# A Fourier-operator tokenizer whose spectra change their order in SBUF: the mix, the prelude and the pair loops

## The reference, cut to what matters

```
spec = DFT of every image, kept modes only (8 x 16 modes, 32 channels, re and im)
mix  = for each mode: spec[image, channels] x weights[mode]        # 128 modes
y    = inverse DFT of mix  +  3x3 convolution of the layer's input
h    = leaky(y + bias)                                             # next layer's input
```

## Time and profile before

| | us |
|---|---|
| median of three runs (lowest, highest) | 7572.34 (7569.57, 7587.36) |
| the profiled execution, its own time | 7572.24 |
| span of the profile | 7570.0 |

### The profile page before, as it was taken

The page is one execution under the profiler, slowest core; times in us unless marked ns, Lnnn a source line. Parts: engine busy times, 40 slices in busy tenths (PEclk is TensorE's granted clock), DMA queues, the critical chain, the costliest instruction groups (busy, mean ns, idle before and its releaser), DMA issues. The chain is left out here.

```text
span 7570.0 us, 260619 instructions
## 1 busy us (share of the span) xinstructions
PE 6734.3 (89%) x107382; PEld 4009.6 (53%) x107382; DVE 4997.2 (66%) x7931; ACT 2567.0 (34%) x4418; POOL 64.7 (1%) x47
## 2 busy tenths in 40 slices
PE   4699997999999899999989999758888888888888
PEld 3566666666666666666654444334444444444443
DVE  3499995777777477777657777665545545454554
ACT  1244442333333233333223333233343333433334
POOL 1000000000000000000000000000000000000000
PEclk8799998999999899999989999879999999999999
DMA  6666665444444444444432222200000000000000
GB/s 169 150 127 125 127 125 131 122 125 118 123 124 114 132 121 125 118 123 124 112 102 77 76 77 77 88 6 1 3 1 3 3 1 3 1 3 3 1 3 2
DMA packets 657148, 581.17 MB, mean 77 GB/s; under 512 B 328160, under 2 KB 527968, under 8 KB 649190
## 3 DMA queue, kind: packets, MB, share of 16 engines
q1 hardware_dynamic: 656776, 576.22, 31.0%
HBM read 328.55 MB, written 260.39 MB: 78 GB/s over the span
## 5 line engine op out<-in xcount | busy, mean ns | idle before, releaser
L554 PE MATMUL abank<-inv_basis,mode_tile 128*32 128x128 f32 x32768 | 1013.8, 276 | 84.9 <-DMA mode_tile<-m_img 56.6
L600 PE MATMUL zbank<-rows_in,conv_taps 64*32 64x512 f32 (+1 forms) x18432 | 1057.0, 588 | 6.1 <-issue 4.9
L554 PEld LDWEIGHTS abank<-inv_basis,mode_tile 128*32 128x32 f32 x32768 | 877.3, 111 | 259.8 <-issue 259.8
L961 DVE SCALAR_TENSOR_TENSOR rows_out<-zbank,conv_bias,work 128x1024 f32<-128x1024 f32 x512 | 633.9, 1279 | 524.9 <-PE zbank L609 510.0
L822 ACT ACTIVATE turned<-tbank 128x1024 f32<-128x1024 f32 x400 | 410.4, 1026 | 1560.3 <-PE tbank L623 1560.2
L816 ACT ACTIVATE inv_copy<-abank 128x1024 f32<-128x1024 f32 x512 | 524.4, 1024 | 766.6 <-PE abank L554 766.6
L638 PE MATMUL zbank<-fwd_basis,turned 128*64 128x128 f32 x12288 | 758.1, 276 | 19.4 <-ACT turned L822 14.7
L937 DVE TENSOR_TENSOR work<-inv_copy 128x512 f32<-128x512 f32 x1024 | 654.2, 685 | 155.1 <-ACT inv_copy L816 154.8
L638 PEld LDWEIGHTS zbank<-fwd_basis,turned 128*64 128x64 f32 x12288 | 666.5, 137 | 96.9 <-issue 96.9
L609 PE MATMUL zbank<-rows_in,conv_taps 32*32 32x512 f32 (+1 forms) x18432 | 702.5, 593 | 0.0
L600 PEld LDWEIGHTS zbank<-rows_in,conv_taps 64*32 64x32 f32 x18432 | 347.7, 106 | 578.5 <-issue 562.8
(11 more groups left out here) (367 smaller groups left out, 7103.8 us busy)
## 6 DMA issues: line engine op xcount, KB each, us to landing
h_rows<-rows_out SPq DMA_DIRECT2D x768, 256.0 KB, 4.0
rows_in<-h_rows SPq DMA_DIRECT2D x384, 512.0 KB, 4.9
m_img<-rows_out SPq DMA_DIRECT2D x32, 1024.0 KB, 5.4
mode_tile<-m_img SPq DMA_DIRECT2D x512, 64.0 KB, 2.9
rows_in<-x_slots SPq DMA_DIRECT2D x96, 194.9 KB
rows_out<-x_slots SPq DMA_DIRECT2D x96, 194.9 KB
x_slots<-x_pad SPq DMA_DIRECT2D x4, 3121.5 KB
tokens<-spectra SPq DMA_DIRECT2D x512, 4.0 KB
```

Of the source, the lines that this page charges most:

```text
L554: last = nc.tensor.matmul(ab[32 * p:32 * p + 32, s, 128 * k:128 * k + 128], mode_tile[u][:, k, a, :], inv[:, k, s, 128 * p:128 * p + 128], ...
L600: nc.tensor.matmul(section(zb[32 * p:32 * p + 32, 2 * a + so, :])[:, :, :, out], conv_t[part, dx, so, :], moving(part, p, 0, src), start=( ...
L961: nc.vector.scalar_tensor_tensor(out=rows_out[u][:, half].rearrange("p (s x) -> p s x", s=2), in0=zb[:, 2 * a:2 * a + 2, :], scalar=conv_b ...
```

## The change

1. `g_img` is ordered by mode: the 128 images of one mode are adjacent. The stationary operand of L773 becomes contiguous. The writers of `g_img` (L836, the expansion's copies L902 and L1063) write one word out of each 128.
2. The weights of mix step `a + 3` are asked for right after the store of step `a - 1`; in the first layer those of steps 1 to 3 ahead of the mix.
3. The last store of a mix is split: eight partitions first, with a semaphore of their own (`m_head`), and the modes of pair 0 wait for that head and for the seven stores ahead of it.
4. In the prelude each tile has a modes buffer of its own (in `rows_flat`), so L921 does not wait for stores; the grid's `x_modes` are asked for after tile 1.
5. The four copies to `x_slots` are gone. `x_rows` come straight from `x_pad`, as 12 transfers of 3 partitions in place of 3 of 12.
6. The pair loops have no hint.

```diff
-        g_img = spectra[:].rearrange("p (n m) -> p n m", n=IMGS)
+        g_img = spectra[:].rearrange("p (m n) -> p n m", n=IMGS)
...
-        modes_out = [inv_copy[0][:, u, :] for u in range(2)]
+        modes_out = [rows_flat[:, MODES * t:MODES * t + MODES] for t in range(ET)]
...
-            return nc.Fori(start, end, engines=bass.OrderedEngineSet([eng.engine]),
-                           hint_back_edge=eng.engine == mybir.EngineType.PE)
+            return nc.Fori(start, end, engines=bass.OrderedEngineSet([eng.engine]))
...
         def sp_slot(sp, slot):
-            sp.wait_ge(pad_stored, 16 * ET)
-            sp.dma_start(x_slots[:, slot, :, :], x_pad[:, rows, :, start:start + RUN]).then_inc(slots_stored, 16)
...
-                if t == 3:
+                if t == 1:
                     sp_grid_modes(sp)
...
             for dx in range(3):
-                sp.dma_start(x_rows[u][32 * dx:32 * dx + 12, :, 0:SPAN],
-                             x_slots[bass.ds(2 * n, 2), :, :, dx:dx + SPAN].rearrange("a r c x -> (r c) a x"))\
-                    .then_inc(x_rows_in[u], 16)
+                for r in range(4):
+                    at, start = 32 * dx + 3 * r, ROW_START[r] + dx
+                    sp.dma_start(x_rows[u][at:at + 3, :, 0:SPAN],
+                                 x_pad[bass.ds(2 * n, 2), ROW_SET[r], :, start:start + SPAN].rearrange("a c x -> c a x"))\
+                        .then_inc(x_rows_in[u], 16)
...
+            if a == 7:
+                sp.dma_start(m_img[0:8, :, a, :], mixed[a % 4][0:8, :].rearrange("p (k x) -> p k x", k=4)).then_inc(m_head, 16)
...
+            if kind == "first":
+                for a in range(1, 4):
+                    sp_load_weights(sp, l, a)
             for a in range(8):
-                if a >= 4 or (a >= 1 and kind == "first"):
-                    sp_load_weights(sp, l, a)
...
                 if a >= 1:
                     sp_store_mixed(sp, l, a - 1)
+                if 1 <= a <= 4:
+                    sp_load_weights(sp, l, a + 3)
...
-            for v in range(4):
+            for v in range(3):
                 sp.wait_ge(m_stored[v], 16 * 2 * (l + 1))
...
+            sp.wait_ge(m_stored[3], 16 * (2 * l + 1))
+            sp.wait_ge(m_head, 16 * l + 16)
             sp_load_modes(sp, 0, 0)
...
-                need(act, g_stored[t % 2], 16 * (t // 2))
-                nc.scalar.activation(modes_out[t % 2], zb[:, 2 + t % 2, :], ACT.Identity).then_inc(g_ready, 1)
+                nc.scalar.activation(modes_out[t], zb[:, 2 + t % 2, :], ACT.Identity).then_inc(g_ready, 1)
```

More of the change, by code:

```diff
@@ L126, in build_tokenizer @@
         grid_pad = scratch("grid_pad", (2, 3, PLANE))
-        x_slots = scratch("x_slots", (IMGS, 4, 3, RUN))
         grid_slots = scratch("grid_slots", (4, 3, RUN))
@@ L168, in build_tokenizer @@
         h_stored = [sem(f"h_stored{u}") for u in range(2)]
-        g_stored = [sem(f"g_stored{u}") for u in range(2)]
+        g_stored = sem("g_stored")
         q1_done = sem("q1_done")
@@ L182, in build_tokenizer @@
         m_stored = [sem(f"m_stored{v}") for v in range(4)]
+        m_head = sem("m_head_stored")
         NP = PAIRS // 2
@@ L227, in build_tokenizer @@
         tile_s = lambda t: t if t < 2 else (t - 2) // 3
-        XSTORES = 16 * (ET // 2)
         x_tiles = x_pairs.rearrange("n (a p) x -> p (n a) x", a=2)
@@ L260, in sp_store_spectrum @@
                 sp.dma_start(grid_spec[3 * t:3 * t + 3, :, :].rearrange("p r m -> p (r m)"),
-                             modes_out[t % 2][0:3, :]).then_inc(g_stored[t % 2], 16)
+                             modes_out[t][0:3, :]).then_inc(g_stored, 16)
             else:
-                sp.dma_start(x_spec[:, t - 2, :, :].rearrange("g r m -> g (r m)"), modes_out[t % 2][:])\
-                    .then_inc(g_stored[t % 2], 16)
+                sp.dma_start(x_spec[:, t - 2, :, :].rearrange("g r m -> g (r m)"), modes_out[t]).then_inc(g_stored, 16)
         def sp_slot(sp, slot):
             start, rows = ROW_START[slot], ROW_SET[slot]
-            sp.wait_ge(pad_stored, 16 * ET)
-            sp.dma_start(x_slots[:, slot, :, :], x_pad[:, rows, :, start:start + RUN]).then_inc(slots_stored, 16)
             sp.dma_start(grid_slots[slot, :, :], grid_pad[rows, :, start:start + RUN]).then_inc(slots_stored, 16)
@@ L318, in sp_grid_modes @@
         def sp_grid_modes(sp):
-            for u in range(2):
-                sp.wait_ge(g_stored[u], 16)
+            sp.wait_ge(g_stored, 16 * 2)
             for g in range(4):
@@ L331, in sp_embed_stores @@
                 sp_store_spectrum(sp, t)
-                if t == 3:
+                if t == 1:
                     sp_grid_modes(sp)
             sp.wait_ge(pad_stored, 16 * ET)
-            for u in range(2):
-                sp.wait_ge(g_stored[u], XSTORES)
+            sp.wait_ge(g_stored, 16 * ET)
             for g in range(4):
@@ L428, in sp_store_mixed @@
             sp.wait_ge(zeroed, NZERO)
-            sp.dma_start(m_img[:, :, a, :], mixed[a % 4].rearrange("p (k x) -> p k x", k=4)).then_inc(m_stored[a % 4], 16)
+            if a == 7:
+                sp.dma_start(m_img[0:8, :, a, :], mixed[a % 4][0:8, :].rearrange("p (k x) -> p k x", k=4)).then_inc(m_head, 16)
+            rest = 8 if a == 7 else 0
+            sp.dma_start(m_img[rest:, :, a, :], mixed[a % 4][rest:, :].rearrange("p (k x) -> p k x", k=4))\
+                .then_inc(m_stored[a % 4], 16)
         def sp_mix(sp, l, kind):
+            if kind == "first":
+                for a in range(1, 4):
+                    sp_load_weights(sp, l, a)
             for a in range(8):
-                if a >= 4 or (a >= 1 and kind == "first"):
-                    sp_load_weights(sp, l, a)
                 if kind == "first" and a in (1, 2, 3, 4):
@@ L442, in sp_mix @@
             if kind == "first":
-                sp.wait_ge(slots_stored, 16 * 8)
+                sp.wait_ge(slots_stored, 16 * 4)
                 sp_grid_rows(sp, 0)
@@ L452, in sp_mix @@
             sp_store_mixed(sp, l, 7)
-            for v in range(4):
+            for v in range(3):
                 sp.wait_ge(m_stored[v], 16 * 2 * (l + 1))
                 sp.wait_ge(zeroed, NZERO)
+            sp.wait_ge(m_stored[3], 16 * (2 * l + 1))
+            sp.wait_ge(zeroed, NZERO)
+            sp.wait_ge(m_head, 16 * l + 16)
+            sp.wait_ge(zeroed, NZERO)
             sp_load_modes(sp, 0, 0)
+            sp.wait_ge(m_stored[3], 16 * 2 * (l + 1))
+            sp.wait_ge(zeroed, NZERO)
             if kind == "first":
@@ L536, in _ @@
             nc.gpsimd.memset(conv_bd[:], 0.0).then_inc(zeroed, 1)
-            nc.gpsimd.memset(rows_flat[:], 0.0).then_inc(zeroed, 1)
+            nc.gpsimd.memset(rows_flat[:, MODES * ET:], 0.0).then_inc(zeroed, 1)
             nc.gpsimd.memset(rows_flat_out[:], 0.0).then_inc(zeroed, 1)
@@ L561, in pe_x_conv @@
             pe_need(pe, z_free, 2 * n)
-            pe.wait_ge(x_rows_in[u], 48 * (i + 1))
+            pe.wait_ge(x_rows_in[u], 192 * (i + 1))
             pe.nop(nofuse=True)
@@ L900, in mix @@
                         for g in range(2):
-                            at = 128 * (32 * g + 4 * i)
-                            last = nc.scalar.activation(spectra[:, at:at + CH], xbank[i % 2][g], ACT.Identity)
+                            at = 32 * g + 4 * i
+                            last = nc.scalar.activation(g_img[:, at:at + 4, :], xbank[i % 2][g].rearrange("p (n m) -> p n m", n=4),
+                                                        ACT.Identity)
                         last.then_inc(expand_act, 1)
@@ L1061, in mix @@
                         for g in range(2, 4):
-                            at = 128 * (32 * g + 4 * i)
-                            last = nc.vector.tensor_copy(spectra[:, at:at + CH], xbank[i % 2][g])
+                            at = 32 * g + 4 * i
+                            last = nc.vector.tensor_copy(g_img[:, at:at + 4, :], xbank[i % 2][g].rearrange("p (n m) -> p n m", n=4))
                         last.then_inc(expand_dve, 1)
```

## The result

The changed kernel took 7610.27 us, the median of five runs (7598.89 to 7616.55), against 7576.78 (7569.57 to 7587.36) for the kernel before, now also of five. The recorded ratio is 1.0039, 95% interval 1.0026 to 1.0053, that is 20 to 40 us (the two medians alone give 1.0044, 33 us). The forecast was 7573, in a range of 7400 to 7800, with 0.46 for slower. The profiled execution took 7603.24 us, its span 7601.3.

A forecast was written before the change was run, and what follows sets the result against it. TensorE and VectorE were taken as near their limits in layer 0, TensorE in middle layers, with weight and modes waits in the mixes. Terms -19 - 52 + 4 - 84 + 160 - 8 = +1 on 7572.24 gave 7573 us, range 7400 to 7800.

The forecast's parts named there:

- prelude -19: Prelude: removing ScalarE's 22.4 us wait for a store gains 22.4, slower expansion copies cost 3; together -19 us.
- first mix -52: First mix: 127 us falls to 72 to 75 with contiguous operand, earlier weights and no slot copies; bounds -35 and -70.
- three later mixes -84: Later mixes: each falls from 80 us to 50 to 52, -28 each; bounds -13 and -38.
- The modes copies' +160: Pair loops: strided writes make eight copies 0.90 us longer a pair; 58 us in layer 0, 102 in middle layers.
- the 4 set aside for layer 0's start: Start of layer 0: pair 1's x_rows take twelve issues instead of three, ahead of its modes; +4 us (0 to 8).
- The loops' -8: Pair loop exits: four stalls, some 7.6 us together, vanish without the hint; -8 us (bounds 0 and -8).
- +3 (bounds 0 and 7.2): Prelude's expansion: copies writing one word in 128 cost ScalarE 0.90 us more a step, about covered; +3 us.
- the first case: Whole kernel: the sum of terms holds as made, 7520 to 7630 us; chance 0.38.
- The strided write costs nothing: Rival, modes copies: the write has no price, the gains stand alone, 7413 us; chance 0.26.
- TensorE stalls at the loops' back edges: Rival, pair loops: without the hint each back edge costs 1.2 to 2.7 us, +110, 7683 us; chance 0.16.
- Layer 0 becomes bound by a few DMA engines: Rival, layer 0: three engines carry each x_rows transfer, 11.8 to 23.9 us a pair; 7743 us at the middle; chance 0.20.
- the two rates: DMA-engine rival: an engine moves 23 GB/s as in the second mix, or 11.4 as in layer 0.

The follow-up runs named there:

- order by image: The changed kernel with the spectra put back in their old order, all else as changed; 7464.74 us, ratio 0.9858.
- hint back: The changed kernel with the hint of TensorE's pair loops put back; 7615.33 us, ratio 1.0056.
- Runs of 2: The changed kernel with the spectra ordered in pairs of adjacent modes; 7408.98 us, ratio 0.9783.
- runs of 4: The changed kernel with the spectra ordered in groups of four adjacent modes; 7474.31 us, ratio 0.9852.
- rows early: Kernel with spectra in pairs of modes, plus grid rows and pair 0's x_rows issued after step 5's store in the first mix; 7415.66 us, ratio 0.9780.
- order alone: The kernel before with only the new by-mode order of the spectra and its two expansion writers; 7730.31 us, one run.

## Why the forecast came out as it did

**Held.** That gains and the price of the strided write nearly cancel: the sum was +1, the two profiles are 31 us apart, 14 without the blocks. The terms, forecast and measured: prelude -19 and -15.5; first mix -52 and -51.2; three later mixes -84 and -95.7. The modes copies' +160 is +185 when the changed kernel's three layers are set against those of order by image; against the kernel before the three layers grew by 54.8 and 118.6, in all 173, the 4 set aside for layer 0's start included, since they lost the hint too. The loops' -8 was some -16 by hint back. The rule of the Trainium skill on cachelines ("SBUF — State Buffer", the section on the DMA port swizzle) foretold that a write which changes its line at each word pays; the trace agrees, 395 against 268 ns. The same note of the Trainium skill wants at least two hits on a line for full bandwidth. Runs of 2 agree on both sides (281 ns, 3.77 us a step), and runs of 4 for the read, which there has one hit to a line (7.47 us).

**Mis-sized.** "If a write goes at that pace, an instruction of 128 elements grows by 128 x (1.71 - 0.83) = 112 ns, from 268 to 380": it grew by 127, or 0.99 ns a word. The later mixes gained 4 us more each than the DMA rate I assumed allowed: steps 4 to 7 took 3.9 us each instead of 5, at 270 GB/s and a share of 0.85, while steps 0 to 3 took 19.6 instead of 16. And for the expansion, "+3 (bounds 0 and 7.2)" was 5.2: ScalarE and VectorE both write word by word there, on 128 partitions, and start a copy of 512 words every 1.14 us (two in 2.27 us), which is more a word than the modes copies need. One sum has a slip: the small ends of the gains' terms add up to some -70, not -95, so the first case should have reached to 7660.

**Right sum, wrong way.** The first mix: I had 57 us of steps and 15 behind them. It was 35 and 41, so that this term came out right is luck. SP's list of late constants (the last store issued 23 us behind the last matmul) and the 15 us from there to the modes (10.5 of them for the `x_rows` ahead, by rows early) took what the matmuls gave back.

**The rivals.** "The strided write costs nothing" fell with order by image. "TensorE stalls at the loops' back edges" fell with hint back. The rule of the Trainium skill that stood beside it ("Runtime: NRT & Kernel Launch", instruction fetch, that a branch breaks the sequential prefetch) did not show here: no wait of the matmuls for issue stands in the first middle layer of the changed kernel (1258 to 2470 us). "Layer 0 becomes bound by a few DMA engines" did not come about: with three-partition transfers in order by image a layer takes 900.9 us, no more than before. In the trace of the changed kernel the 72 packets of a pair's `x_rows` take 421 ns on average where they took 987, and the set is in after 11 to 12 us instead of 6.5. The packets' records in the two traces settle the rival's premise. From 400 to 1100 us, three of these packets are under way at once for 398 us and more than three for 6.5; before, twelve are for 235 us and more than twelve for 21.5. So a set is carried by three engines, at 24 x 0.421 = 10 us of each in a pair of 15.1: the premise held, and the rate kept it from deciding (8316 bytes in 0.421 us are 20 GB/s an engine, near the upper of the two rates). Its cost appeared once, where nothing hides it, as 10.5 us between the head and the modes of the first mix (13.8 us in runs of 2, 3.3 in rows early).

**Open.** The stretches between a layer's last inverse and the next mix grew by 9 us in all, which the forecast did not have. It goes with the word-by-word write: 106.1, 105.8 and 109.1 us in the three kernels that have it (changed, hint back, order alone), 95.3 to 99.4 in the others. Three sets of modes copies, each 1.0 us longer, stand in such a stretch; that they are all of it is not shown. The blocks' scatter of 35 us follows TensorE's granted clock, as said above, but what lowers the clock in one execution more than in another is not explained, and it is as large as the result.

## What to carry to other kernels

When a layout makes one reader contiguous, count its writers: here 1024 matmuls became faster by 0.11 us each, in four short stages, and 1536 writes slower by 0.127 us on the path of 192 pairs. Before choosing between two orders, look for a third in between; runs of two words nearly gave both ends their full pace. And a faster engine gains nothing in a ring that it is not part of: the order alone gave the mix 5 us of 80, the earlier weights 13, both together 32.

## What the runs showed of the hardware

A contiguous 128-column fp32 stationary operand went at 112 ns a matmul (3.57 us over 32), every second word at 118, every fourth at 233, one in 128 at 219, all at a granted clock of 1.00. ScalarE's copy of 32 x 128 took 268 ns contiguous, 269 in runs of four words, 281 in runs of two, 395 word by word. When ScalarE and VectorE both wrote 128 x 512 word by word, each needed some 2.2 ns a word (1.14 us a copy), against the 1.8 of ScalarE's copies of 32 x 128 (0.83 + 0.99); whether the second engine or the 128 partitions make the difference is not shown. Loads of three partitions put three packets under way at a time, loads of twelve put twelve.
